# A graph layer and a feed-forward layer on one core: the edges into the first 256 nodes as a dense matrix

## The chip, the core and the metric

The kernel runs on one core of a Trainium2 chip. The metric is the device time of one execution in microseconds (us). The engines are named PE (TensorE), DVE (VectorE), ACT (ScalarE), POOL (GpSimd) and SP (SyncE).

## What is computed

There are 6250 nodes of 256 float32 features and 100,000 weighted edges, sorted by their target node `dst`. The targets are drawn as 6250·u², so they crowd at low node numbers: of the inputs timed here 20,448 edges end in nodes 0 to 255. The sources `src` are spread evenly over all nodes. With `f` the layer-normed rows of `x`:

```python
def _gcn(x, W, b, src, dst, w, n):
    h = x @ W
    return segment_sum(w[:, None] * h[src], dst, n) + b
# graph part, added to x
h  = _gcn(f, W1, b1, src, dst, edge_weight, N)
y  = leaky(concat([h, f[root]], 1))
y  = leaky(_gcn(y, W2, b2, src, dst, edge_weight, N))
x1 = x + leaky(concat([y, h[root]], 1) @ Wl + bl)
# feed-forward part on layernorm(x1): a router picks the best half of the
# nodes; those get gelu(t @ fw1 + fb1) @ fw2 + fb2, times their router weight
```

Since the sum over edges and the product with W can change places, the kernel sums rows first: each of the two graph layers adds up w · row[src] for each target, of `f` in layer 0 and of `y @ W2` in layer 1.

## The kernel before, in words

**Edges as tiles.** The edges are cut into 784 tiles of 128 (`NT`), in the order of `dst`. Four tiles make a group (`TG`), four groups a round (`QG`, `RING` = 16 tiles): 49 rounds (`NIT`) a layer, from the last edges to the first. Nodes are cut into 49 windows of 128 (`NW`). For each tile POOL issues one indirect DMA (L434) that gathers its 128 source rows of 1 KB into the ring in SBUF; DVE makes a selection matrix S of 128×128 (L1153: a column number equals the target within the window, times the edge's weight); PE multiplies S with the rows, four tiles into one PSUM sum (L716, two instruction records a tile); DVE adds the sum to the window's accumulator `acc` (L1161). Where a group's targets reach into the next lower window, it is done again with shifted targets (`S_more`, `dmore`; one extra each time).

**Far tiles.** In every third round one of the 16 tiles is not gathered by POOL. SP fetches its 128 rows with 128 DMAs of one row (L348, in `far_tile`), whose addresses it reads from a table in four loads of 32 registers (L343). PE waits for the tile at its group (`far_ready`, set at L355). There are 16 such tiles a layer and two slots for them.

**Steps.** Once the targets of a window are complete, a step s works on it. In layer 0 a step copies the sum out (ACT, L522), turns it (PE, L789), multiplies it with W1 and W2 (L813, L804) and lets ACT store 128 rows to DRAM (L541); DVE does `z_step0` in the first group of a round and `zero_step0` in the third. In layer 1 a step is the last product, the residual, the layernorm and half of a feed-forward pass over two windows (L854, L865). Steps begin in round `first` (a value computed on the chip, 1 for these inputs), one a round, each engine's pieces tied to the groups of the round (`steps[q]`); those that are left are done behind the rounds.

**Order.** Each engine runs its own stream in order, and semaphores tie them. DVE selects two groups ahead (`select_ahead`), loads a group's window and number of extras from a table into registers (L1180), adds the group before (`add_last`), then frees the ring slot (`group_used`, L1188), for which POOL waits (8 slots of a group, `SLOTS`). PE's sums alternate between two PSUM banks. Between the layers DVE patches the first gathered round with two late windows (L1344), while SP loads `x` again (L331).

Of the kernel before, what the change touches and what calls it, by code (L numbers as in the profile page):

```python
# [17 lines left out]
def gnn_ffn_kernel(nc, x, src, dst, edge_weight, W1, b1, W2, b2, Wl, bl, root_idx,  # L18
# [3 lines left out]
    ds = bass.ds  # L22
# [12 lines left out]
    TG = 4  # L35
    GE = TG * P
    QG = 4
    RING = QG * TG
    SLOTS = 2 * QG
    PADT = RING  # L40
    NIT = -(-E // (RING * P))
    NT = NIT * RING
    NG = NIT * QG
    GR = NG // 2
    CH = 2 * TG
    CR = NT // CH
    SPARE = NT - -(-E // P)
    RAWG = 8
    FAR_EVERY, FAR_Q = 3, 1
    FARS = (NIT - 1) // FAR_EVERY  # L50
    FAR_SLOTS = 2
    FAR_PASS = 32
# [3 lines left out]
    FIRST_EDGE = (NIT - 1) * RING * P  # L56
# [19 lines left out]
    assert NT == CH * CR and NG == 2 * GR and CR == GR <= P and SPARE < TG and 96 < GR and E > 97 * CH * P  # L76
    assert NIT == FARS * FAR_EVERY + 1 and FARS % 2 == 0 and (NW + 1) << CBITS < 1 << SBITS and RAWG < FAR_EVERY * QG
    assert NIT == NW and NACC <= 1 << CBITS

    f_dram = nc.dram_tensor("normed_rows", (NPAD, D), f32).ap()  # L80
# [3 lines left out]
    with ctx:  # L84
# [14 lines left out]
        ring = sb("ring", [P, SLOTS * TG + FAR_SLOTS, D])  # L99
        far = sb("far", [FARS, P], i32)  # L100
        iota = sb("iota", [P, 2 * P], i16)
        idx = sb("idx", [P, NT], i32)
        dstc = sb("dstc", [P, PADT + NT])
        wc = sb("wc", [P, PADT + NT])
        dmore = sb("dmore", [P, TG])
        idx_far = sb("idx_far", [P, FIRST_TILES], i32)
# [41 lines left out]
        wtab = acc[0:1, 1, 0:NG].bitcast(i32)  # L148
        lag = sb("lag", [1, 1], i32)
# [11 lines left out]
        g_lo = stage[:, 0:NG].bitcast(i32)  # L161
        g_hi = rows[:, 0:NG].bitcast(i32)
# [32 lines left out]
        diag = hT[:, :, :].rearrange("p c n -> p (c n)")[:, 0:4 * GR].rearrange("p (a r c) -> p a r c", a=2, c=2)  # L195
# [8 lines left out]
        up_flat = ps_up[:, :, :].rearrange("p c n -> p (c n)")  # L204
        patch_banks = [[up_flat[:, 0:512], up_flat[:, 512:1024]], [ps_h[:, :], ps_o[:, :]]]
# [16 lines left out]
        dve_chain, far_chain = sem("dve_chain"), sem("far_chain")  # L222
# [41 lines left out]
        near_loaded, near_ready, far_listed, zero_stored = sem("near_loaded"), sem("near_ready"), sem("far_listed"), sem("zero_stored")  # L264
        patch_done, patched = sem("patch_done"), [sem(f"patched{q}") for q in range(QG)]
        x_again = sem("x_again")
        raw_stats, raw_second = sem("raw_stats"), sem("raw_second")
# [36 lines left out]
        def _(sp):  # L304
# [24 lines left out]
            def load_x_again():  # L329
# [4 lines left out]
                for r0, r1 in PART:  # L334
                    sp.dma_start(xs[r0:r1, X0 + NW - 1, :], x[(NW - 1) * P + r0:(NW - 1) * P + r1, :]).then_inc(x_again, 16)
# [1166 lines left out]
```

## Time and profile before

| | |
|---|---|
| time of three executions | 2972.7, 2970.2, 2953.6 us, median 2970.2 |
| span of the profiled execution, its own time | 2915.3 us |
| mean granted clock of PE | 0.808 |
| PE / DVE / POOL / ACT busy | 1865.9 / 1169.0 / 1474.9 / 369.1 us |
| records of PE MATMUL / indirect gathers of POOL | 7011 / 1532 |
| bytes moved by DMA | 244.27 MB, mean 84 GB/s |

The span runs from the first to the last instruction; what lies around it in a timed execution is not in the profile. Busy is the union of an engine's instructions; register, branch, semaphore and DMA-issuing instructions are not in it, so an engine can be taken up and not busy. "issue" is time for which the profile shows no wait. A letter q behind an engine means its queue or sequencer.

### The profile page before, as it was taken

How to read it: one execution, taken by the hardware profiler on the slowest of the kernel's cores; microseconds unless marked ns; L12 is line 12 of the kernel's file. 1: busy time of each engine (PE TensorE's matmuls, PEld its weight loads, DVE VectorE, ACT ScalarE, POOL GpSimd, SP SyncE). 2: the span in 40 equal slices, each digit the busy share in tenths (PEclk: the TensorE clock that was granted, in tenths of full speed). 3: DMA queues.
4: the chain of work that ended last, by engine and by line, in shares of the span. 5: the costliest groups of instructions: out<-in, count | busy, mean ns of one | idle time of the engine just before them, and what ended most of it. 6: DMA issues, size and time to landing. Idle time of an engine off the chain costs nothing.

```text
span 2915.3 us, 49425 instructions
## 1 busy us (share of the span) xinstructions
PE 1865.9 (64%) x7011; PEld 1437.8 (49%) x7012; DVE 1169.0 (40%) x4136; ACT 369.1 (13%) x927; POOL 1474.9 (51%) x1571
## 2 busy tenths in 40 slices
PE   0465646655555556354637888886777686757687
PEld 0344535434443444333526666665666465645475
DVE  6543333332332332222324455444544434434356
ACT  4200000000000000000101111111111111111111
POOL 5455555554555554455344555555555554545430
PEclk9788778777776776767878889988988888978797
DMA  6422222222222322222432222222222222222212
GB/s 202 131 83 81 80 80 80 84 78 74 82 81 78 88 79 75 70 79 77 152 98 72 72 72 81 78 79 75 78 81 76 81 71 69 83 62 82 67 50 88
DMA packets 120873, 244.27 MB, mean 84 GB/s; under 512 B 32822, under 2 KB 71046, under 8 KB 120748
## 3 DMA queue, kind: packets, MB, share of 16 engines
q0 software_dynamic: 73664, 200.90, 24.0%
q1 hardware_dynamic: 35612, 32.02, 3.5%
q10 hardware_dynamic: 11472, 10.27, 1.1%
q14 instruction: 117, 0.96, 0.1%
q8 instruction: 8, 0.13, 0.0%
HBM read 223.42 MB, written 19.64 MB: 83 GB/s over the span
## 4 chain that ended last, share of the span: by engine, by line
SPq 53%; issue 35%; PE 5%; DVE 3%; DVEq 1%; another core or an unknown queue 1%; DMA 1%; ACT 1%; ACTq 0%
SPq L348 45%; SPq L343 7%; PE ps_agg L716 2%; PE ps_dn L854 1%; PE ps_up L865 1%; DVE fw2s L1062 1%; DVE S L1153 0%; ACT xs L480 0%; DVE ring L1442 0%; DMA normed_rows<-xs 0%; DVEq L1193 0%; PE ps_o L804 0%; DVE acc L1161 0%; PE ps_dn L852 0%
## 5 line engine op out<-in xcount | busy, mean ns | idle before, releaser
L716 PE MATMUL ps_agg<-ring,S 128*128 x3136 | 912.1, 440 | 677.0 <-SPq L355 320.3
L716 PEld LDWEIGHTS ps_agg<-ring,S 128*128 128x128 f32 x3136 | 669.1, 221 | 860.1 <-issue 757.8
L434 POOL DMA_INDIRECT ring<-conv_rows,idx x752 | 714.5, 950 | 632.4 <-DVEq L1188 424.2
L434 POOL DMA_INDIRECT ring<-normed_rows,idx x736 | 701.1, 953 | 631.7 <-DVEq L1188 426.7
L1153 DVE TENSOR_SCALAR S<-iota,dstc,wc 128x128 f32<-128x128 int16 x1584 | 454.9, 353 | 377.1 <-issue 360.3
L1161 DVE TENSOR_TENSOR acc<-acc,ps_agg x490 | 206.3, 421 | 893.4 <-PE ps_agg L716 478.4
L716 PE MATMUL ps_agg<-ring,S_more 128*128 x768 | 265.7, 506 | 254.6 <-DVE S_more L1153 150.0
L716 PEld LDWEIGHTS ps_agg<-ring,S_more 128*128 128x128 f32 x768 | 187.6, 254 | 321.3 <-issue 287.9
L854 PE MATMUL ps_dn<-fw2s,hT 128*128 128x256 f32 x848 | 232.7, 434 | 0.0
L854 PEld LDWEIGHTS ps_dn<-fw2s,hT 128*128 128x128 f32 x848 | 179.4, 218 | 49.5 <-issue 21.7
L865 PE MATMUL ps_up<-xnT,fw1s 128*128 128x256 f32 x800 | 195.0, 400 | 8.9 <-issue 7.1
L865 PEld LDWEIGHTS ps_up<-xnT,fw1s 128*128 128x128 f32 x800 | 160.7, 204 | 34.5 <-issue 8.1
L1153 DVE TENSOR_SCALAR S_more<-iota,dmore,wc 128x128 f32<-128x128 int16 x384 | 112.7, 365 | 41.2 <-issue 29.2
L522 ACT ACTIVATE stage<-acc 128x256 f32 (+1 forms) x98 | 40.8, 416 | 541.5 <-DVEq L1192 384.0
L532 ACT ACTIVATE xnT<-ps_t 128x256 f32<-128x256 f32 x49 | 18.8, 383 | 611.9 <-PE ps_t L789 480.2
L568 ACT ACTIVATE hT<-ps_up,fb1c 128x256 f32<-128x256 f32 (+1 forms) x212 | 81.9, 472 | 92.2 <-PE ps_up L865 48.6
L548 ACT ACTIVATE yT<-ps_h,b1c 128x128 f32<-128x128 f32 x98 | 30.6, 363 | 326.9 <-remote 245.6
L1143 DVE SCALAR_TENSOR_TENSOR zT<-yT 128x256 f32<-128x256 f32 x99 | 42.1, 425 | 73.9 <-issue 67.9
L789 PE MATMUL ps_t<-ident,stage 128*128 128x128 f32 x196 | 44.9, 317 | 32.4 <-issue 17.2
L804 PE MATMUL ps_o<-W2s,zT 128*128 128x256 f32 x196 | 64.5, 458 | 0.0
L604 ACT ACTIVATE xn<-rows,norm 128x256 f32<-128x256 f32 x48 | 28.8, 600 | 281.7 <-DVE norm L1377 151.0
L813 PEld LDWEIGHTS ps_h<-xnT,W1s 128*128 128x128 f32 x392 | 55.7, 205 | 4.1 <-ACT xnT L532 0.7
(248 smaller groups left out, 1077.2 us busy)
## 6 DMA issues: line engine op xcount, KB each, us to landing
ring<-normed_rows SPq DMA_DIRECT2D x2048, 1.0 KB
ring<-conv_rows SPq DMA_DIRECT2D x2048, 1.0 KB
ring<-conv_rows,idx POOLq DMA_INDIRECT x752
ring<-normed_rows,idx POOLq DMA_INDIRECT x736
conv_rows<-rows ACTq DMA_DIRECT2D x49, 128.0 KB
xs<-in_x SPq DMA_DIRECT2D x6, 640.0 KB
out_rows<-xs SPq DMA_DIRECT2D x3, 1024.0 KB
xs<-in_x SPq DMA_DIRECT2D x2, 1280.0 KB
```

The costliest lines, as they stand in the source:

```text
L343: _, offsets = nc.values_load_multi_w_load_instructions(bass.at_runtime_partition(far[0:1, c * FAR_PASS:(c + 1) * FAR_PASS], k), engines=( ...
L348: sp.dma_start(ring[p:p + 1, SLOTS * TG + b, :].bitcast(i8), rows_of[ds(offsets[i], D * 4)].unsqueeze(0)).then_inc(far_landed[l][b], 16)
L434: pool.indirect_dma_start(out=ring[:, slot * TG + t, :], out_offset=None, in_=rows_of, in_offset=bass.IndirectOffsetOnAxis(ap=at, axis=0)) ...
L568: last = nc.scalar.activation(hT[:, b * HB + c, 0:tokens], ps_up[:, c, 0:tokens], ACT.Gelu_apprx_tanh, bias=fb1c[:, b * HB + c:b * HB + c ...
L716: last = nc.tensor.matmul(to, select[:, t, :], moving, start=(t == 0), stop=(t == TG - 1))
L789: last = nc.tensor.transpose(ps_t[:, k * P:(k + 1) * P], stage[:, k * P:(k + 1) * P], ident[:, :])
L804: last = nc.tensor.matmul(ps_o[:, 0:D], zT[:, k, :], W2s[:, k, :], start=False, stop=(k == KC - 1))
L813: last = nc.tensor.matmul(ps_h[:, c * P:(c + 1) * P], W1s[:, k, c * P:(c + 1) * P], aggT[:, k, :], start=(k == 0), stop=(k == KC - 1))
L854: last = nc.tensor.matmul(ps_dn[:, 0:D], hT[:, c, window * P:(window + 1) * P], fw2s[:, c, :], start=False, stop=(c == HC - 1))
L865: last = nc.tensor.matmul(ps_up[:, c, 0:tokens], fw1s[:, k, (b * HB + c) * P:(b * HB + c + 1) * P], of[:, k, :], start=(k == 0), stop=(k = ...
L1153: last = V.tensor_scalar(to[:, t, :], iota[:, 0:P], at, wc[:, ds(column, 1)], ALU.is_equal, ALU.mult)
L1161: V.tensor_tensor(to, to, flat(ps_agg[:, ds((i + 1) & 1, 1), 0:D]), op=ALU.add).then_inc(acc_step[l], 1)
```

## The change

**Tiles.** The first 160 tiles (`NM`) are taken out of the rounds. Half a tile of padding (`LEAD`) is put ahead of the edges, so that these tiles hold exactly the edges up to node 255. 624 tiles are left: 52 rounds (`NIT`) of three groups (`QG`), with a ring of 6 groups. Far tiles and all of `far_tile` go; POOL gathers all 624 (622 with edges).

**Matrix.** The 160 tiles become a matrix A of 256 targets by all source nodes, held in `xs` (which ACT clears once its rows are stored). In rounds 1 to 40 of layer 0 DVE makes two one-hot matrices for each of four tiles (`hot_tile`: 128×128 of the source within its window, 128×245 of target offset and source window, times the weight), PE multiplies them (`build_tiles`, behind the third group), and a round later DVE adds the 128×245 result to A at a target read from a table (`add_tile`). Rounds 41 to 50 take A and `f` in ten chunks of five windows: SP loads the rows, DVE copies A's chunk (1280 columns a partition), PE makes ten products of 128×128 by 128×256 (`dense_chunk`), and DVE adds them to windows 0 and 1 (`add_chunk`). A is stored to DRAM (6.5 MB in five DMAs of SP). In layer 1 each round begins with one block of A and one window's rows, two DMAs of 128 KB by SP, two products on PE (`dense_block`) and one addition of 512 columns on DVE (`add_block`).

**Rest.** `first` is at least 4 (computed 6 for these inputs, so 46 steps lie in the rounds and two behind them). SP, not ACT, stores a step's rows in layer 0 (`store_rows`). ACT, not SP, loads `x` again, after the patches; DVE waits for it only before the steps. In layer 1 `conv_step1` and `ffn_step_b` share the third group. `select_ahead` comes behind the group's addition, not ahead of it. Should a tile span five targets or more, a general path (`rare_edges`) is taken: 160×49 single products a layer.

```diff
-    QG = 4
+    QG = 3
+    NIT = NW + 3
+    NM = NT - NIT * RING
+    MW = 2
+    SPAN = 5
+    KEYS = SPAN * NW
+    BPER = 4
+    CHUNK = 5
...
 # SP
-            def far_tile(l, rows_of, n, b, before):
-                ...
-                    for i in range(FAR_PASS):
-                        sp.dma_start(ring[p:p + 1, ...], rows_of[ds(offsets[i], D * 4)]...)
+            def store_rows():
+                sp.wait_ge(o_kept[0], s + 2)
+                sp.dma_start(t2_dram[ds(at, P), :], rows[:, :]).then_inc(t2_stored, 16)
+            for i in range(PIECES):
+                sp.dma_start(a_dram[:, w0:w1, :], xs[:, w0:w1, :]).then_inc(matrix_stored, 16)
+            def load_block(i):
+                sp.dma_start(block_a, a_dram[:, a if i < NW else NW, :]).then_inc(block_loaded, 16)
+                sp.wait_ge(t2_stored, 16 * (NW - a + 2))
+                sp.dma_start(block_t, t2_dram[a * P:(a + 1) * P, :]).then_inc(block_loaded, 16)
+            for i in range(1, NIT):
+                sp.wait_ge(block_used, i)
+                load_block(i)
 # ACT
+            act.wait_ge(dense_done, B_IT + CHUNKS)
+            act.wait_ge(matrix_stored, 16 * PIECES)
+            for c, (w0, w1) in enumerate(XCH):
+                act.dma_start(xs[:, X0 + w0:X0 + wf, :], x[w0 * P:wf * P, :]...).then_inc(x_again, 16)
 # PE
+            def build_tiles(it):
+                pe.wait_ge(build_added, it * BPER + (BPER + 1))
+                pe.wait_ge(build_ready, it)
+                for t in range(BPER):
+                    matmul(up_banks[...], src_hot[:, t, :], key_hot[:, t, :])
+            def dense_chunk(it):
+                for m in range(MW):
+                    for k in range(CHUNK):
+                        matmul(to[...], chunk_a[:, k, m * P:(m + 1) * P], blocks[row])
+            def dense_block(it):
+                for m in range(MW):
+                    matmul(to, block_a[:, m * P:(m + 1) * P], block_t)
-            rounds(1, (turn_step1, ffn_step_a, conv_step1, ffn_step_b), ...)
+            rounds(1, ((turn_step1,), (ffn_step_a,), (conv_step1, ffn_step_b)), ...)
 # DVE
+            def hot_tile(it, t):
+                if t == 0:
+                    dve.wait_ge(build_done, it)
+                V.tensor_scalar(src_hot[:, t, :], iota[:, 0:P], src_low[...], None, ALU.is_equal)
+                V.tensor_scalar(key_hot[:, t, :], iota[:, 0:KEYS], keys[...], wc[...], ALU.is_equal, ALU.mult)
+            def add_tile(it, t):
+                base = within(dve.value_load(base_row[0:1, ds(at, 1)]), MSPAN - SPAN)
+                dve.wait_ge(build_done, it)
+                dve.wait_ge(build_added, it * BPER + (t + 1))
+                V.tensor_tensor(to, to, of, op=ALU.add).then_inc(build_added, 1)
             def edge_round(l, it, steps, matrix=None):
                 for q in range(QG):
-                    select_ahead(l, it, q)
                     ... (table load, add_last, group_used)
+                    if matrix == "adds" and q == 0:
+                        with dve.If(it > B_IT):
+                            add_chunk(it, p0 + 2)
                     ... (extras' selections)
+                    select_ahead(l, it, q)
+                    if l == 1 and q == 0:
+                        add_block(p0)
                     ... (window_ready, steps[q])
+                    if matrix and q < 2:
+                        matrix_tiles(it, q, matrix == "adds")
```

## Rows read from the trace of the kernel before

**Rows 1.** The page, part 4: the chain that ended last, by line.

```profile
SPq L348 45%; SPq L343 7%; PE ps_agg L716 2%; PE ps_dn L854 1%; PE ps_up L865 1%; DVE fw2s L1062 1%; DVE S L1153 0%; ACT xs L480 0%; DVE ring L1442 0%; DMA normed_rows<-xs 0%; DVEq L1193 0%; PE ps_o L804 0%; DVE acc L1161 0%; PE ps_dn L852 0%
```

**Rows 2.** The page, part 5: costliest groups, busy, mean, idle before and its releaser.

```profile
L716 PE MATMUL ps_agg<-ring,S 128*128 x3136 | 912.1, 440 | 677.0 <-SPq L355 320.3
...
L434 POOL DMA_INDIRECT ring<-normed_rows,idx x736 | 701.1, 953 | 631.7 <-DVEq L1188 426.7
L1153 DVE TENSOR_SCALAR S<-iota,dstc,wc 128x128 f32<-128x128 int16 x1584 | 454.9, 353 | 377.1 <-issue 360.3
L1161 DVE TENSOR_TENSOR acc<-acc,ps_agg x490 | 206.3, 421 | 893.4 <-PE ps_agg L716 478.4
...
L1153 DVE TENSOR_SCALAR S_more<-iota,dmore,wc 128x128 f32<-128x128 int16 x384 | 112.7, 365 | 41.2 <-issue 29.2
```

**Rows 3.** One line, L348: count, duration ns min/median/max, first and last start.

```profile
L348 SPq DMA_DIRECT2D ring<-normed_rows x2048: 1/225/1390, 88.7 to 1430.6; - x187
...
L348 SPq DMA_DIRECT2D ring<-conv_rows x2048: 2/225/1392, 1459.5 to 2819.3; - x187
```

**Rows 4.** Waits: who waited for whom, us in total, times, longest.

```profile
PE ps_agg L716 <- SPq L355: 320.3, 22, 30.9
```

**Rows 5.** The chain in order of time, 600 to 627 us: start, us, what.

```profile
603.10 2.06 SPq L343
...
607.22 0.22 SPq L348
...
612.96 0.70 SPq L348
```

**Rows 6.** Timeline of POOL, 1108 to 1131: start, us, what, [idle before].

```profile
1114.77 0.94 POOL L434 DMA_INDIRECT ring<-normed_rows,idx  x1 [12.71 <-DVEq L1188]
1116.02 0.94 POOL L434 DMA_INDIRECT ring<-normed_rows,idx  x1 [0.30 <-issue]
```

**Rows 7.** Timeline of DVE, 1406 to 1440 us.

```profile
1408.79 0.42 DVE L1161 TENSOR_TENSOR acc<-acc,ps_agg  x1 [0.38 <-issue]
...
1417.66 0.42 DVE L1161 TENSOR_TENSOR acc<-acc,ps_agg  x1 [3.42 <-issue]
...
1420.15 0.42 DVE L1161 TENSOR_TENSOR acc<-acc,ps_agg  x1 [0.27 <-issue]
...
1425.83 0.42 DVE L1161 TENSOR_TENSOR acc<-acc,ps_agg  x1 [0.39 <-issue]
...
1429.07 0.42 DVE L1161 TENSOR_TENSOR acc<-acc,ps_agg  x1 [0.27 <-issue]
```

**Rows 8.** Stretches: busy us (instructions) of each engine, PEclk, DMA share, GB/s.

```profile
600.00:900.00 300.00, 178.20 (x624) 132.35 (x625) 95.39 (x305) 19.66 (x55) 159.02 (x167) 0.75 0.27 79
...
2811.90:2827.90 16.00, 15.95 (x65) 12.91 (x65) 10.54 (x41) 2.96 (x8) 0.00 (x0) 0.88 0.01 2
2822.40:2838.80 16.40, 16.29 (x78) 13.99 (x77) 10.85 (x41) 4.62 (x12) 0.00 (x0) 1.00 0.00 0
```

**Rows 9.** Timeline of all engines, 608 to 640 us.

```profile
609.16 1.89 PE L716 MATMUL ps_agg<-ring,S 128*128 x8
...
627.09 3.78 PE L716 MATMUL ps_agg<-ring,S 128*128 x8 [1.40 <-DVE acc L1161]
...
629.56 0.29 DVE L1321 COPY acc<-vrow 128x256 f32 x1 [0.36 <-issue]
...
630.36 1.03 POOL L434 DMA_INDIRECT ring<-normed_rows,idx  x1 [0.30 <-issue]
```

**Rows 10.** Timeline of POOL, 1430 to 1500 us.

```profile
1445.30 0.95 POOL L434 DMA_INDIRECT ring<-conv_rows,idx_far  x1 [29.58 <-DMA conv_rows<-rows]
```

**Rows 11.** Timeline of SP, 1440 to 1500 us.

```profile
1459.51 40.46 SPq L348 DMA_DIRECT2D ring<-conv_rows  x47
```

**Rows 12.** Timeline of DVE, 1456 to 1505 us.

```profile
1487.49 0.69 DVE L1344 TENSOR_TENSOR ring<-ring,ps_o 128x512 f32<-128x512 f32 x1 [11.88 <-remote]
```

**Rows 13.** One line, L1180: DVE’s table load at each edge group.

```profile
L1180 DVEq TENSOR_LOAD <-acc x392: 3/305/716, 84.3 to 2836.4; - x196
```

More of the change, by code:

```diff
@@ L513, in rounds @@
                 with act.Fori(0, stop) as s:
-                    for q in range(QG):
-                        steps[q](s)
+                    for piece in steps:
+                        piece(s)
             def stage_sums(l, s):
@@ L748, in rounds @@
+            def rounds(l, steps, stop, ahead_of_steps):
                 pe.reg_mov(extras, 0)
                 pe.reg_mov(step, 0)
-                d = within(pe.snap(first), NIT, 1)
-                with pe.Fori(0, d) as it:
-                    for q in range(QG):
-                        edge_group(l, it, q)
-                if ahead_of_steps is not None:
-                    ahead_of_steps()
+                d = within(pe.snap(first), NIT, NIT - NW + 1)
+                if l == 0:
+                    with pe.Fori(0, 1) as it:
+                        edge_round(l, it, None, None, False)
+                with pe.Fori(1 - l, d) as it:
+                    edge_round(l, it, None)
+                ahead_of_steps()
@@ L765, in rounds @@
                     with pe.Fori(done, stop) as s:
-                        for q in range(QG):
-                            steps[q](s)
-            def no_step(s):
-                pass
+                        for group in steps:
+                            for piece in group:
+                                piece(s)
             def first_root_term():
@@ L781, in _ @@
             pe.sem_inc(raw_second, 1)
[L782 removed]
+            pe.reg_mov(first, pe.value_load(lag[0:1, 0:1], min_val=NIT - NW + 1, max_val=NIT))
             def turn_sums(l, s):
@@ L1242, in rounds @@
                         s = within(dve.snap(step), NIT)
-                        edge_round(l, it, [lambda piece=piece: piece(s) for piece in steps])
+                        edge_round(l, it, [lambda piece=piece: piece(s) for piece in steps], matrix)
                         dve.reg_mov(step, s + 1)
-                end = within(dve.snap(within(dve.snap(extras), NG * NW) + NG), NG * (NW + 1))
+                with dve.Else():
+                    rare_edges(l)
+                end = within(dve.snap(within(dve.snap(extras), NG * NW) + NIT * PER[l]), MOST)
                 done = within(dve.snap(step), NIT - 1)
```

524 lines of the change are left out of this document (340 added, 184 removed).

## The prediction

> **What bounds the kernel now.** I read the chain that ended last first: SP's line L348, the 128 one-row transfers of a far tile, holds 45% of the span, and no compute engine more than a few per cent [rows 1]. The sources of L348 say what to see there: 2048 transfers in each layer, from 88.7 to 1430.6 us and from 1459.5 to 2819.3 us, that is without a break over both layers [rows 3]. 16 tiles in 1342 us are 83.9 us a tile, and a tile comes every third round: 28.0 us a round in layer 0. The groups and waits say who pays: PE stood 320.3 us before L716 for SP's far tile [rows 2, 4], POOL stood 631.7 us in layer 0, mostly for DVE to free a slot, since DVE stood for PE [rows 2].
>
> A far tile should take less. In a quiet stretch one transfer takes 0.22 us (0.32 with its address move and the gaps) and a table load 2.06 [rows 5]: 128 × 0.32 + 4 × 2.1 = 49 us. But beside POOL's packed gathers SP's instructions take 0.70 us each [rows 5]. DVE shows the same: the first group of a round took 3.24 us from addition to addition in a quiet stretch (1425.83 to 1429.07) and 8.87 us in a slow one (1408.79 to 1417.66, with 3.42 us of "issue") [rows 7]. So there are two costs: SP's queue, and a slowing of SP, DVE and PE's sequencer, whose cause I can't read off with certainty.
>
> Below that lie three floors. **POOL:** one gather every 1.25 us when packed [rows 6], so 16 tiles cost 20 us a round. **PE:** four tiles take 1.89 us at full clock and 3.78 at half [rows 9]; the last rounds of layer 1, with neither gathers nor far rows beside them, keep it busy 15.95 of 16.00 and 16.29 of 16.40 us [rows 8]. **DVE:** three quiet groups of layer 0, among them those with the zeroing and with the first step piece, take 8.92 us (1420.15 to 1429.07) [rows 7].
>
> **The change, part by part.** Far tiles: 4096 transfers go, and with them the 28-us pace. SP gets two 128-KB DMAs a round in layer 1 and one in layer 0; a round later they are needed, so I cost them at nothing (cover: a round; without it some 3 us each).
>
> POOL: 1244 gathers in place of 1532, 12 tiles × 1.25 = 15.0 us a round. Over 52 rounds a layer that is 780 us, a floor and not the pace, as follows.
>
> DVE in layer 0, rounds 1 to 40: three groups 8.9 us. Extras: 384 selections are 96 extras, 48 a layer [rows 2]; cut in threes the inputs have 46, 0.9 a round, each four selections (0.28 us each, as L1153's group busy time per instruction), one addition (0.42) and a shift, 1.7 us: 1.5. Matrix: per tile one selection of 128 columns (0.28), one of 245 (no row; between 0.28 and 0.56, I take 0.40, as only the columns grow), one addition of 245 columns from PSUM (0.42 by L1161) with its table load and waits (a quiet plain group of 2.5 us less its selections and addition leaves some 0.9 for all such work; I take 0.5, between 0 and 0.9): 1.6 us, four tiles 6.4, and 0.8 for branches. Sum 17.6 us. DVE also waits at its first `hot_tile` for PE's products, which stand behind PE's step piece of the third group: 0 to 3 us, I take 1.4. With 1 us for what slowing is left: **20 us a round**, above POOL's 15.0 and PE's (three groups 5.7, extras 1.7, build 1.9, step some 3.3 = 12.6 at full clock, 16 at the 0.75 of [rows 8]).
>
> Rounds 41 to 51 of layer 0: DVE's copies and additions are small, but PE has 20 records more (4.7 us), and DVE's `add_chunk` waits for them: 18.5 us, between POOL's 15.0 and 22.
>
> Layer 1, rounds with a step: PE 16.3 [rows 8], less one group 1.9, plus a dense block 0.95, plus extras 1.7 = 17.1 us at full clock. DVE comes to about 16 (16.0 as in [rows 8], less a group 2.5, plus `add_block` 1.4, plus extras 1.5). Two engines this close wait for one another, now that two PE pieces share the third group: I take **20 us**, between 17.1 and 23. Rounds without a step go at POOL's pace, 16 us.
>
> The lag of 6 leaves two steps behind the rounds of each layer; before there were none. No overlap with gathers: some 7 us each in layer 0, 13 in layer 1 (a round of 16 less three quarters of its edge work), 40 us together.
>
> Between the layers: in the old kernel the third group's patch came at 1474.92 and the fourth's at 1487.49 [rows 12], while POOL had begun those gathers at 1445.30 [rows 10] and packed them: 14 × 1.25 us ends at 1463. They landed beside SP's reload of `x`. Now ten tiles land before the reload. From layer 0's last group (some 6 us after SP's last row at 1430.6 [rows 3]) to layer 1's first (some 9 us after the last patch) it was 60 us; I take 10 off. The bounds are 25 off and, if the reload is felt in the rounds, nothing.
>
> SP stores rows where ACT did: one semaphore more in a chain that has a round's time; nothing. Storing A (6.5 MB, five DMAs) and ACT's clearing of `xs` are once each; under 10 us, inside the 18.5 above.
>
> **The sum**, against the profiled execution: layer 0's rounds begin at 84.3 us [rows 13]; first round with set-up 25; 41 × 20 = 820; 10 × 18.5 = 185; two steps 14: 1128. Between the layers 50: 1178. Layer 1: 6 × 16 = 96; 46 × 20 = 920; two steps 26; the tail as before, from the end of the last round (two us behind the last table load at 2836.4 [rows 13]) to 2915.3, 77: 1119. Span 2297 us, against 2915.3. The median of the runs lies 54.9 above the profiled span; kept, that gives **2350 us**, 21% less.
>
> **A rule against the change.** The copy of 256 columns at 629.56 took 0.29 us; the gather that began at 630.36 took 1.03 us, where others take 0.95 [rows 9, 6]. The Trainium skill, "SBUF — State Buffer", section "SBUF: two separate sides", says a float32 copy within SBUF on VectorE locks GpSimd out of writing DMA descriptors; by it the ten `copy_chunk` of 1280 columns, each five times the row's 0.29 us, would stop POOL for up to 15 us in all, and the sum would stay, since POOL has slack there.
>
> **Rivals.**
>
> *The slowing belongs to the gathers, not to SP's rows.* For: it starts and ends with POOL's packed stretches, in the middle of ordinary work of DVE. Against: POOL had been packed from 1445.30 [rows 10] without harm to its neighbours until SP began at 1459.51, and SP then needed 40.46 us for 47 transfers [rows 11], 0.86 each. And POOL will now be paced by fours, with 5 us of gathers in a 6.7-us group. If it stays, I add 3.5 us to each of 51 rounds of layer 0 and 2.5 to each of 46 of layer 1: 179 + 115 = 294, so 2640 us. The Trainium skill, "Perfetto Trace Analysis", section "DMA Instruction — HWDGE (DVE, Sync)", says that these two sequencers share the block that makes descriptors; by that rule DVE's slow stretches would go with SP's transfers, and the time would be that of the forecast. That PE's sequencer is slowed too speaks against its being all.
>
> *The engines overlap better than I allow.* Rounds fall to their bare sums, 17.6 and 17.1: 41 × 2.4 + 10 × 2 + 46 × 2.9 = 252 less, 2100 us. For: PE ran without a gap in the tail [rows 8]. Against: it had no extras there.
>
> *Slower: DVE's matrix work in the slow mode.* Place: DVE's stream in rounds 1 to 40. Price: the slow group is 8.87/3.24 = 2.7 times the quiet one [rows 7]. If POOL, freed of SP's pace, packs its gathers through the whole round, 17.6 us become 48, and layer 0 alone grows by 41 × 28 = 1150 us over the forecast: 3500 us. It decides from 27 us a round in both layers on, that is if more than a third of DVE's work is slow. Against: POOL can't stay packed while it waits for DVE's slots; the two throttle one another.
>
> *The change doesn't do what it says:* the general path is taken. The inputs' last matrix tile spans nodes 251 to 255, inside the five allowed, so it isn't; otherwise many milliseconds.
>
> **How the numbers follow.** Forecast 0.55; slowing stays 0.25; better overlap 0.13; slow matrix work 0.05; general path 0.01; no change within 1% (what a measurement of this kernel can't tell from none) 0.01. The range goes from the better overlap, 2100, to just over the slowing rival, 2660. Faster 0.93, within 1% 0.01, slower 0.06.
>
> **What the changed profile would show.** The chain no longer held by SP but by DVE and PE in turns; L434 with 1244 gathers, no idle time ended by SP; windows of layer 0 with rounds of 20 us, then 18.5, and of layer 1 with 20; PE's granted clock over 0.85 in layer 1; SP's and DVE's 0.70-us instructions gone. Wrong if gathers at 1.25 us fill 95% of a layer (then POOL's floor is the pace), if DVE's "issue" time grows beyond the 377 us of L1153 (the slowing stays), or if DVE waits over 3 us a round at `hot_tile` for `build_tiles`.

## The result

| kernel | median us | lowest to highest | ratio to before, 95% |
|---|---|---|---|
| before | 2971.45 | 2953.6 to 2976.29 | |
| after | 2483.58 | 2475.5 to 2491.61 | 0.838 [0.834, 0.842] |

16% faster. The forecast was 2350 us in a range of 2100 to 2660: right in sign and range, 134 us too low. The profiled execution of the kernel after took 2479.38 us, 1.8 us more than its span.

The page of the kernel after: busy times, the chain by engine, then the groups that answer to [rows 2].

```profile
PE 1820.0 (73%) x7053; PEld 1422.3 (57%) x7054; DVE 1209.6 (49%) x4253; ACT 376.1 (15%) x930; POOL 1205.6 (49%) x1280
...
PE 26%; issue 17%; DVE 14%; DVEq 14%; another core or an unknown queue 4%; POOL 1%; ACT 0%; DMA 0%; ACTq 0%
...
L780 PE MATMUL ps_agg<-ring,S 128*128 (+1 forms) x2496 | 713.4, 437 | 309.8 <-DVE acc L1287 140.5
L484 POOL DMA_INDIRECT ring<-conv_rows,idx x612 | 582.1, 951 | 576.2 <-DVEq L1390 390.4
...
L1287 DVE TENSOR_TENSOR acc<-acc,ps_agg x406 | 170.8, 421 | 604.3 <-issue 268.3
L1279 DVE TENSOR_SCALAR S<-iota,dstc,wc 128x128 f32<-128x128 int16 x1264 | 362.4, 363 | 176.9 <-issue 175.1
```

SP, 52% of the chain by its two lines in [rows 1], has no share left. PE's wait for SP (320.3 us, [rows 4]) is gone, and its idle time before the sums falls from 677 to 310 us. PE and DVE take turns, as forecast, and POOL waits for DVE's slots. But "issue" at DVE's selections is still 175 us (360 before), and 268 at its additions.

Two stretches of 300 us, in the columns of [rows 8]: one of layer 0, one of layer 1.

```profile
600.00:900.00 300.00, 217.04 (x812) 168.03 (x811) 152.41 (x502) 26.95 (x75) 167.74 (x175) 0.80 0.29 82
1300.00:1600.00 300.00, 241.00 (x950) 191.85 (x951) 145.69 (x532) 50.68 (x132) 146.25 (x154) 0.88 0.27 79
```

PE has 217 us of work here where [rows 8] had 178, and POOL is busy 168 of 300 us. No engine is full, so the round is a chain through several.

### The profile page after: what moved, and what is told of

Same layout as the page of the kernel before. It is cut to its first block, busy times and chain, and to the rows that moved or that the text cites. A ratio compares the mean times of both kernels' runs of the same rounds, so it can differ in the third digit from the quotient of the medians.

```text
span 2477.6 us, 40334 instructions
## 1 busy us (share of the span) xinstructions
PE 1820.0 (73%) x7053; PEld 1422.3 (57%) x7054; DVE 1209.6 (49%) x4253; ACT 376.1 (15%) x930; POOL 1205.6 (49%) x1280
## 3 DMA queue, kind: packets, MB, share of 16 engines
q0 software_dynamic: 59808, 163.13, 22.7%
## 4 chain that ended last, share of the span: by engine, by line
PE 26%; issue 17%; DVE 14%; DVEq 14%; another core or an unknown queue 4%; POOL 1%; ACT 0%; DMA 0%; ACTq 0%
PE ps_agg L780 11%; PE ps_dn L979 6%; DVE S L1279 4%; PE ps_up L990 3%; DVEq L1279 2%; DVEq L1377 2%; DVEq L1395 2%; DVE acc L1296 1%; DVEq L1391 1%; DVE S_more L1279 1%; DVEq L1287 1%; PE ps_agg L847 1%; PE ps_dn L977 1%; PE ps_o L1023 1%
## 5 line engine op out<-in xcount | busy, mean ns | idle before, releaser
L780 PE MATMUL ps_agg<-ring,S 128*128 (+1 forms) x2496 | 713.4, 437 | 309.8 <-DVE acc L1287 140.5
L484 POOL DMA_INDIRECT ring<-conv_rows,idx x612 | 582.1, 951 | 576.2 <-DVEq L1390 390.4
L484 POOL DMA_INDIRECT ring<-normed_rows,idx x600 | 576.6, 961 | 489.4 <-DVEq L1390 338.2
L780 PEld LDWEIGHTS ps_agg<-ring,S 128*128 128x128 f32 x2496 | 535.5, 220 | 445.4 <-issue 360.2
L1287 DVE TENSOR_TENSOR acc<-acc,ps_agg x406 | 170.8, 421 | 604.3 <-issue 268.3
L1279 DVE TENSOR_SCALAR S<-iota,dstc,wc 128x128 f32<-128x128 int16 x1264 | 362.4, 363 | 176.9 <-issue 175.1
L780 PE MATMUL ps_agg<-ring,S_more 128*128 (+1 forms) x736 | 264.5, 522 | 215.6 <-DVE S_more L1279 179.6
L780 PEld LDWEIGHTS ps_agg<-ring,S_more 128*128 128x128 f32 x736 | 185.3, 262 | 284.5 <-issue 250.2
L1296 DVE TENSOR_TENSOR acc<-acc,ps_agg 128x512 f32<-128x512 f32 x52 | 35.7, 686 | 157.3 <-PE ps_agg L780 80.5
L813 PE MATMUL ps_up<-hT 128*128 128x245 f32 x320 | 74.4, 375 | 0.0
L1341 DVE TENSOR_TENSOR xs<-xs,ps_up 128x245 f32 x160 | 64.9, 406 | 18.0 <-issue 14.8
```

The lines of the kernel that those rows point to most:

```text
L484: pool.indirect_dma_start(out=ring[:, slot * TG + t, :], out_offset=None, in_=rows_of, in_offset=bass.IndirectOffsetOnAxis(ap=at, axis=0)) ...
L780: last = nc.tensor.matmul(to, select[:, t, :], moving, start=(t == 0), stop=(t == TG - 1))
L813: last = nc.tensor.matmul(up_banks[:, t // 2, t % 2 * KEYS:(t % 2 + 1) * KEYS], src_hot[:, t, :], key_hot[:, t, :], start=True, stop=True)
L1279: last = V.tensor_scalar(to[:, t, :], iota[:, 0:P], at, wc[:, ds(column, 1)], ALU.is_equal, ALU.mult)
L1287: V.tensor_tensor(to, to, flat(ps_agg[:, ds((i + 1) & 1, 1), 0:D]), op=ALU.add).then_inc(acc_step[l], 1)
L1296: V.tensor_tensor(first_acc, first_acc, flat(ps_agg[:, ds((i + 1) & 1, 1), :]), op=ALU.add).then_inc(acc_step[1], 1)
```

## The rounds in every profile

A round here lasts from its first table load on DVE (L1180 in [rows 13], L1377 after) to that of the next; us, means. The last column counts DVE's queue instructions (register, branch, semaphore; no table loads) that took 0.65 to 0.76 us, of some 9,800. Before has 49 rounds of 16 tiles, after 52 of 12; "layer 1" leaves out its first six rounds. The third column is the median of the kernel before in the same comparison.

```
kernel            span    before beside it  layer 0, rounds 6-40  41 on   layer 1   slow on DVE
before            2915.3  (2971)            28.19                 26.60   27.53     577
after             2477.6  2971              20.70                 20.91   22.81     271
b0_before         2976.3  2966              28.76                 27.21   28.36     582
b1_no_far         2647.6  2906              24.70                 23.32   25.38     590
b2_half           2152.9  2906              19.67                 17.77   19.54      92
e2_no_build       2469.5  2966              19.69                 21.41   23.68     281
e7_sp_rows        2489.7  2966              20.68                 20.93   23.07     299
e1_pool_far       2106.3  2071              19.53                 19.90   19.57       0
c1_after          2039.8  2071              15.58                 15.82   20.43       0
e5_half_gathers   2038.0  2071              15.65                 15.19   20.50       0
e8_block_late     1907.1  2071              15.67                 15.06   17.51       0
e9_both_late      1892.3  2071              15.62                 13.89   17.50       0
```

The table holds the chief surprise. The experiments came on five chips, of two kinds: on two the kernel before takes 2906 and 2966 us, on three 2070 to 2071. I call them the slow and the quick kind. Each chip was met in one comparison only, so whether the kind stays with the chip is not shown. The first comparison (2971), and so the result, is of the slow kind. They differ in the last column.

The table also shows how far a column can be trusted. On the quick kind, c1_after and e8_block_late run the same layer 0 and stand at 15.82 and 15.06 in rounds 41 to 50. On the slow kind, after and e2_no_build run the same layer 1 and take 22.81 and 23.68.

## The experiments

### The change on a quick chip

**c1_after** is the kernel after, unchanged.

> The kernel after, unchanged, on the chip of this comparison. Where the kernel before takes about 2071 us, theory (layer 0 is then at GpSimd's 12 x 1.25 = 15 us a round, layer 1 at the 20.3 us of the run with ScalarE's stores, since that run differs from this in layer 0 alone): 2020 to 2045 us, 1 to 3% faster than before. Rival (the stores cost ScalarE's path in layer 0): 1990 to 2015 us. Where the kernel before takes about 2970 us: 2475 to 2495 us.

Measured: 2037.26 us, ratio 0.982 [0.979, 0.986], inside the 2020 to 2045 of its text. So the same change is worth 16% on one kind of chip and 1.8% on the other. One line, L1377, of the first profile and then of this one (count, duration ns min/median/max, first and last start):

```profile
L1377 DVEq FUSED_REGOPS  x204: 4/65/699, 138.8 to 2380.3; - x102
```

```profile
L1377 DVEq FUSED_REGOPS  x204: 57/65/71, 122.3 to 1942.6; - x102
```

The same 204 register instructions have the same median, but on the quick chip none is over 71 ns, and on the slow kind some take 699. Over the program, 271 of 9833 instructions of DVE's queue and 129 of 7335 of PE's are slow in the first, none in the second. DVE's tensor work is nearly equal (1209.6 and 1195.1 us busy). The two executions differ by 438 us of span.

The slow instructions are not the whole of this difference. In rounds 6 to 40 of layer 0, which take 20.70 us and 15.58, DVE's queue instructions take 9.9 us a round and 7.8, PE's 5.7 and 4.9. But PE's products take 14.8 us a round and 12.6, at a granted clock of 0.80 and 0.93. No run takes the clock's part from the rest. Where a price in us a round is put on the slowing below, it is the whole difference between the two chips.

**e4_act_stores** gives the stores back to ACT.

```diff
-                sp.wait_ge(o_kept[0], s + 2)
-                sp.dma_start(t2_dram[ds(at, P), :], rows[:, :]).then_inc(t2_stored, 16)
+                act.wait_ge(o_kept[0], s + 2)
+                act.dma_start(t2_dram[ds(at, P), :], rows[:, :]).then_inc(t2_stored, 16)
```

> The kernel after, with ScalarE waiting for and storing each node tile's rows itself in layer 0, as before the change. My step costed this move at nothing beside the rounds' other work: one transfer and one wait per round on an engine that is busy under 20% of the span. Theory: no difference, 2475 to 2495 us. Rival (ScalarE's next stage stands behind the wait for its own copy, and TensorE behind the stage): 0.3 to 0.8 us in each of 52 rounds, 2500 to 2525 us.

Measured: 2039.39 us, on a quick chip, 2 us from c1_after on another one (before 2070.85 and 2071.05 beside them). Nothing, as costed. Its ratio is 0.987 [0.982, 0.993]; the absolute figures of its text were for the other kind.

### What bounds before and after on a quick chip

**e1_pool_far**: the kernel before, with SP's tiles gathered by POOL.

```diff
-                    by_sp = q == FAR_Q and it > 0 and it % FAR_EVERY == 0
+                    by_sp = False
-                if q == FAR_Q:
-                    pe.wait_ge(far_ready[l], ((it * 171) >> 9) + 1)
 # SP: the far_tile calls go
```

> The kernel before with one thing changed: GpSimd gathers all sixteen tiles of every round, and SyncE fetches no tile row by row. No matrix of far nodes, nothing else of the change. Theory (SyncE's one-row transfers set the rounds before, and the change gains by taking them away): GpSimd now has 16 gathers x 1.25 us = 20.0 us per round as its floor against 15.0 in the kernel after, rounds of 21.5 to 24 us, 104 of them and some 190 us around them: 2430 to 2690 us, most likely 2500, so nearly all of the gain is had without the matrix. Rival (the slowed instructions come with GpSimd's packed queue, not with SyncE's rows): a GpSimd that is the bound is packed all the time, every instruction of VectorE and TensorE's queue goes slow, 2700 to 2950 us.

Measured: 2107.19 us, ratio 1.017 [1.016, 1.019], on a quick chip. The text was written for 2970 us and so can't be judged by its times. But 36.3 us more fits 32 gathers of 1.25 us (40 us), and the rounds stand at 19.5 us. Two lines of it, one per layer:

```profile
L427 POOL DMA_INDIRECT ring<-conv_rows,idx x768 | 738.5, 962 | 235.6 <-issue 229.0 <-DVEq L1179 6.6
L427 POOL DMA_INDIRECT ring<-normed_rows,idx x752 | 717.6, 954 | 248.7 <-issue 219.7 <-DVEq L1179 29.1
```

In layer 0 POOL waits for DVE 29.1 us, where [rows 2] had 426.7, and in layer 1 6.6: it is the bound, always packed, and yet no queue instruction of DVE is slow. Packed gathers alone don't slow the queues. It takes the chip too.

**e5_half_gathers**: the kernel after with half the gathers.

```diff
-                    for t in range(TG):
+                    kept = 2 if it >= 3 else TG
+                    for t in range(kept):
...
-                        pool.indirect_dma_start(...).then_inc(landed[slot // QG][q], 16)
+                        pool.indirect_dma_start(...).then_inc(landed[slot // QG][q], 16 * TG // kept)
```

> The kernel after, with GpSimd issuing two of the four gathers of each group from round 3 of each layer on; what TensorE multiplies for the other two tiles is what the ring held, all else stays. Theory (layer 0's rounds on a quiet chip are GpSimd's 15 us; layer 1's are the chain through the block's product): on a chip where before takes 2071 us, layer 0's rounds fall from 15.7 to 12 to 14.5 us, layer 1's stay within 1 us: 100 to 190 us less than the kernel after. On a chip where before takes 2970 us the packed stretches are half as long, the 0.70-us instructions nearly vanish: 2000 to 2150 us. Rival (VectorE's and TensorE's own work sets the rounds in both layers): less than 50 us gained on the quiet chip.

Measured: 2040.23 us on a quick chip, against 2037.26. My theory fell and its rival stands: layer 0's 15.6 us lie next to POOL's 15.0, but come from DVE and PE. The change had already freed POOL.

### The wait in layer 1

The timeline of the kernel after at a round's start in layer 1, all engines:

```profile
1689.02 3.72 PE L979 MATMUL ps_dn<-fw2s,hT 128*128 128x256 f32 x16
...
1692.58 1.03 PE L847 MATMUL ps_agg<-blocks 128*128 128x256 f32 x4
1695.39 0.69 DVE L1296 TENSOR_TENSOR acc<-acc,ps_agg 128x512 f32<-128x512 f32 x1 [5.72 <-PE ps_agg L780]
...
1696.28 0.42 ACT L582 ACTIVATE stage<-acc 128x256 f32 x1 [6.84 <-DVEq L1408]
...
1696.75 0.44 PE L911 MATMUL ps_t<-ident,stage 128*128 128x128 f32 x2 [1.42 <-ACT stage L582]
```

PE ends the last step piece of the round before (3.72 us), and only then makes the block's product. DVE waits for it with nothing to do ahead of that, idle for 5.72 us. (The row names PE's next group, L780, whose semaphore came 0.30 us behind the block's; the wait in the code is for the block's product, and in c1_after the profile puts all 45 such waits down to L847.) Behind its addition stand `window_ready` and the step piece, for `window_ready` ACT, and for ACT's stage PE. So **e8_block_late** moves the addition down:

```diff
-                    if l == 1 and q == 0:
-                        add_block(p0)
                     if steps and q == 0:
-                        dve.wait_ge(acc_step[l], p0 + 2)
+                        dve.wait_ge(acc_step[l], p0 + 2 - l)
                         dve.sem_inc(window_ready[l], 1)
                     if steps:
                         steps[q]()
+                    if l == 1 and q == 0:
+                        add_block(p0)
```

> The kernel after; in layer 1 alone VectorE opens the window for the node tile's steps and does its step piece ahead of adding the block's product, in place of behind it. Theory (layer 1's rounds of 22.8 us hold a chain of its own: TensorE's last step piece, then the block's product, then VectorE's wait of 5.7 us for it, then ScalarE's stage, then TensorE's turn): the wait leaves the path, rounds of 20 to 21.3 us in 45 rounds, 2375 to 2420 us. Rival (the round is set by the sum of the work and the waits of the twelve gathered tiles, so the wait only moves): 2465 to 2490 us.

Measured: 1915.66 us on a quick chip, 0.927 [0.923, 0.930], 122 us less than c1_after (I had expected 64 to 109 less, for the slow kind), and 124 less than e4_act_stores on the same chip. Layer 1's rounds fall from 20.43 to 17.51 us, layer 0's stay. The addition's idle time in c1_after, then in this run:

```profile
L1296 DVE TENSOR_TENSOR acc<-acc,ps_agg 128x512 f32<-128x512 f32 x52 | 35.7, 686 | 125.5 <-PE ps_agg L847 125.5
```

```profile
L1296 DVE TENSOR_TENSOR acc<-acc,ps_agg 128x512 f32<-128x512 f32 x52 | 35.7, 687 | 47.8 <-PE ps_agg L847 38.4 <-DVE mv L1603 9.4
```

**e9_both_late** moves the dense chunk's addition in layer 0 behind the step piece as well:

```diff
-                    if matrix == "adds" and q == 0:
-                        with dve.If(it > B_IT):
-                            add_chunk(it, p0 + 2)
...
-                        if l == 0:
-                            dve.wait_ge(dense_added, it + 2)
...
                     if l == 1 and q == 0:
                         add_block(p0)
+                    if matrix == "adds" and q == 0:
+                        with dve.If(it > B_IT):
+                            add_chunk(it, p0 + 2)
```

> As the run with the block's addition behind the step piece in layer 1, and in layer 0 also the addition of the dense chunk moved behind the step piece (rounds 41 to 52). Theory: beside the gain of the first, ten rounds of layer 0 lose VectorE's wait of 4.5 us for the dense chunk, 1 to 3 us of each: 10 to 35 us less than that run, 2340 to 2400 us. Rival (layer 0's rounds 41 to 50 are no longer than rounds 6 to 40 for another reason than this wait): no difference from that run within 8 us.

Measured: 1895.97 us, 0.916 [0.914, 0.918], 20 us less than e8_block_late; rounds 41 to 50 fall from 15.1 to 13.9 us, more than the 0.8 us by which two runs of the same code differed there, and to 13.8 in the second run below. That is 12 of the 20 us. This version beats both kernels. In the stretches of layer 1 PE is now nearly full at full clock; one of c1_after, then one of this run:

```profile
1250.00:1550.00 300.00, 258.62 (x1091) 208.11 (x1092) 163.13 (x612) 63.47 (x168) 163.18 (x172) 0.95 0.30 87
```

```profile
1300.00:1600.00 300.00, 288.62 (x1325) 241.17 (x1324) 190.41 (x715) 81.46 (x209) 198.67 (x208) 1.00 0.36 106
```

I ran it once more, as **e9_again**, hoping for a chip of the slow kind:

> The version with both additions moved behind the step piece once more, for a chip on which the kernel before takes about 2900 to 2970 us; on a chip of 2071 us it took 1896. Theory (the 5.7-us wait for the block's product is on the path there too, and queue instructions of 0.70 us come on top as in the kernel after): layer 1's rounds of 22.8 us fall to 20 to 21, layer 0's rounds 41 to 50 from 20.9 to 19.5 or less, 2340 to 2410 us beside 2484, a ratio to before of 0.79 to 0.81. Rival (on such a chip VectorE is the late engine, so that what is taken from its waits is filled with its slowed instructions): 2440 us or more. On a chip where before takes 2071 us: 1890 to 1905 us again.

It came on a quick one: 1903.85 us, 0.920 [0.916, 0.923]. What it brings where before takes 2970 us is not known.

### What the slow kind of chip makes of it

**b0_before**: the kernel before, for its profile.

> The kernel before as it was; only two loads of one number, once per layer, are written with their bounds. It is run for its profile, since the kernel before takes 2071 us on the chips of these experiments and 2970 in the first comparison. Theory (the instructions of 0.70 us of SyncE, VectorE and TensorE's queue belong to the chip, not to the kernel): at about 2071 us there are fewer than 30 of them on SyncE and on VectorE, where the first profile has 665 and 628; a round of 16 tiles lasts GpSimd's gathers, 19 to 19.8 us, where it lasted 28.2; and the run with SyncE's tiles given to GpSimd is longer by just those gathers, 34 x 1.25 = 42 us (36 measured). Rival (the instructions are as slow as before and something else is faster): their counts are above 300 each. At about 2970 us: all is as in the first profile.

It came on a slow chip: one execution, 2978.44 us, rounds as in the first profile, 582 slow instructions on DVE. (The 665 and 628 of its text are those over 0.55 us on SP and DVE, table loads among them; counted as in the table they are 516 and 577.) So there is no profile of before on a quick chip, and that POOL bounds it there rests on e1_pool_far.

**b1_no_far**: no far tiles at all, by anyone.

```diff
 # SP's far_tile calls and PE's wait go, as in e1_pool_far; POOL goes on leaving those tiles out
-                if q == FAR_Q:
-                    pe.wait_ge(far_ready[l], ((it * 171) >> 9) + 1)
```

> The kernel before with SyncE's tiles left out altogether: neither SyncE nor GpSimd fetches the last tile of group 1 in every third round, and TensorE multiplies what its ring slot holds. GpSimd's gathers are as many as before. On a chip where the kernel before takes about 2970 us, theory 1 (the chain of waits runs through SyncE's rows, 320 us of TensorE's wait being for them): 2400 to 2600 us. Theory 2 (the 0.70-us instructions of VectorE and TensorE's queue, which come with GpSimd's packed gathers, are the price, and the rows are only what is late last): 2750 to 2950 us. On a chip where it takes about 2071 us both expect that GpSimd's 16 x 1.25 us a round stay the bound and the rows were free: 2050 to 2080 us; a rival is that the rows cost there too: below 2030 us.

**b2_half**: the rows stay, POOL's gathers are halved.

```diff
-                    for t in range(TG - 1 if by_sp else TG):
+                    kept = 2 if it >= 3 else TG - 1 if by_sp else TG
+                    for t in range(kept):
```

> The kernel before with SyncE's rows as they are, but GpSimd issuing two gathers of each group of four from round 3 of each layer on (TensorE multiplies what the ring holds in place of the others). On a chip where the kernel before takes about 2970 us, theory 2 (packed gathers make SyncE's, VectorE's and TensorE's queue instructions slow, SyncE's rows among them): the counts of 0.70-us instructions fall by half or more, SyncE's tile of rows is no longer late, rounds of 19 to 24 us, 2050 to 2500 us. Theory 1 (SyncE's rows are slow by themselves): SyncE's chain stays, 2750 to 2950 us. On a chip where it takes about 2071 us, theory (GpSimd's gathers set the round of 19.5 us): VectorE's and TensorE's own work shows, 1750 to 1980 us; rival (they set it already, as in the kernel after, where half the gathers gave nothing): 2040 to 2075 us.

Both on one slow chip, before 2905.57 us. Without the rows: 2645.1 us, 0.912 [0.907, 0.917]. With the rows and half the gathers: 2154.49 us, 0.743 [0.738, 0.747]. The first value lies between the two theories, the second is theory 2's, though SP's tile is still late 15 times. One wait of the run without rows; then of the run with half the gathers the chain by line, and one wait:

```profile
DVE S L1144 <- issue: 405.1, 357, 8.6
```

```profile
SPq L348 25%; PE ps_agg L717 10%; SPq L343 6%; PE ps_dn L855 5%; DVE S L1154 3%; PE ps_up L866 3%; DVE acc L1162 1%; DVEq L1154 1%; DVE S_more L1154 1%; PE ps_dn L853 1%; DVEq L1194 1%; PE ps_o L899 1%; DVEq L1162 1%; DVE fw2s L1063 1%
```

```profile
PE ps_agg L717 <- SPq L355: 189.4, 15, 25.1
```

With SP silent, DVE is as slow as ever: 590 slow instructions against 577 and 582, and 405 us of "issue" before its selections (360.3 in [rows 2]). So SP's transfers don't cause the slowing. With half the gathers they fall to 92 on DVE, from 342 to 33 on PE's queue and from 516 to 162 on SP's, with all of SP's rows in place. SP is still 31% of the chain, but 750 us earlier. On such a chip the slowing comes with POOL's gathers. It grows with how deep they are packed. The table gives the share of DVE's queue instructions over 0.55 us (table loads among them), by the place of the gather that ran (begun within 1.3 us) in a row of gathers less than 1.4 us apart, from 100 us on. The last column is of instructions with no gather begun in the 3 us before them, without the one drain at the program's end:

```
place                 1     2     3     4     5     6     7   8 on   (none for 3 us)
before             .016  .028  .045  .114  .321  .551  .517  .640   .000
after              .009  .020  .027  .049  .206  .339  .386  .494   .000
b2_half            .000  .001  .131  .373     (under ten instructions a column)    .000
e1_pool_far, quick .000  .000  .000  .000  .000  .000  .000  .000   .000
```

**e7_sp_rows**: the kernel after, plus SP's rows in layer 1, at addresses fixed when the program is built.

```diff
+                for p in range(42):
+                    sp.dma_start(ring[p:p + 1, SLOTS * TG, :], t2_dram[(p * 131 + i * 17) % N:..., :]).then_inc(rows_in, 16)
```

> The kernel after, with 42 more transfers of one row each by SyncE in every round of layer 1, into a slot of the ring that nothing reads: as many per 12 tiles as the kernel before had for 16. [...] Rival (the rows themselves hinder GpSimd's gathers or VectorE, and so cost time wherever they run): rounds longer by 2 us and more, over 100 us more. On a chip where before takes 2970 us: over 300 us more, with SyncE at 0.3 to 0.9 us a row.

On a slow chip: 2499.79 us, 0.844 [0.840, 0.848], 16 us more than the kernel after; layer 1's rounds 23.07 against 22.81. I had expected over 300 us. SP's queue, 42 rows to a round:

```profile
1516.04 15.31 SPq L421 DMA_DIRECT2D ring<-conv_rows  x42
```

0.36 us a row, where [rows 11] had 0.86; groups of 42 take 12.9 to 18.6 us. From one transfer's start to the next it is 0.36 us in the mean here and 0.64 in the kernel before. The transfer itself did not get cheaper: its instruction takes 0.25 us in the mean and 0.23 before, and 196 of 2142 took over 0.55 us, before 505 of 4096. What a row saves is the second instruction, the address move (518 of 4096 over 0.55 us before), and the table loads. The 0.3 us a round that these rows cost lie within the spread of layer 1 on this kind of chip.

**e2_no_build**: the making of the matrix is left out, its use stays.

```diff
-                V.tensor_scalar(src_hot[:, t, :], ...)
-                last = V.tensor_scalar(key_hot[:, t, :], ...)
+                    dve.sem_inc(build_ready, 1)
-                V.tensor_tensor(to, to, of, op=ALU.add).then_inc(build_added, 1)
+                dve.sem_inc(build_added, 1)
-                    last = nc.tensor.matmul(up_banks[...], src_hot[:, t, :], key_hot[:, t, :], ...)
-                last.then_inc(build_done, 1)
+                pe.sem_inc(build_done, 1)
```

> The kernel after without the making of the matrix in layer 0's first 40 rounds: VectorE's eight hot tiles and four additions per round and TensorE's four products of them are left out, so the matrix stays as it was cleared; its storing, loading and use as dense chunks and blocks stay. My step priced this making at 6.4 us of VectorE per round. Theory (quiet chip: it lies on the path with VectorE's and TensorE's other work, but GpSimd's 12 gathers of 1.25 us stand right behind it): layer 0's rounds go from 15.6 to 15.0 to 15.2 us, 15 to 30 us less than the kernel after. Rival (the making lies in VectorE's idle time and GpSimd is not near): no change within 8 us. Second rival (GpSimd's spacing can close up below 1.25 us): rounds of 12 to 14 us, 60 to 140 us less. On a chip where before takes 2970 us: rounds from 20.7 to 17 or less, over 150 us less.

On a slow chip: 2467.52 us, 0.831 [0.827, 0.834], 16 us less than the kernel after. Layer 0's rounds go from 20.70 to 19.69 us, where I had written 17 or less.

The 16 us hide two larger numbers. Layer 0 is 40 us shorter (1100.8 against 1141.1). Layer 1, which the edit doesn't touch, is 33 us longer (1291.4 against 1258.4), for a reason that no run shows. The pieces left out had taken 4.2 us of DVE a round, so three quarters of what it is spared DVE spends waiting or slowed: its slow instructions in rounds 1 to 40 rise from 126 to 174. On a quick chip this run was not made.

## Why the forecast was right, and where not

**Right: SP's rows leave, and the chain goes to DVE and PE.** b1_no_far prices the rows at 260 us of 2906, beside the 320.3 us that PE waited for them [rows 4]. That is a little over half of the gain (8.8 of 16.2 points). The rest I put down to fewer and less packed gathers; no run shows that at twelve tiles a round. By layers, first load to first load and to the end: 1411.6 to 1141.1 us, and 1419.4 to 1258.4.

**The cause of the slowing was named wrongly.** I priced what is left of it at 1 us a round in layer 0 and at nothing in layer 1, and gave the rival, that it belongs to the gathers, 0.25. Its mechanism holds (b1_no_far, b2_half). By after against c1_after it costs 5.1 us a round in layer 0 and 2.4 in layer 1, near the rival's prices: 3.5 on top of my 1 in layer 0, and 2.5 in layer 1. The lower clock of PE is in these numbers. What spoke against it for me, POOL packed without harm from 1445.30 [rows 10], was between the layers. The part about pacing holds: gathers at the fifth place or deeper fell from 470 to 327, the slow instructions of DVE from 577 to 271.

My signs for it were poor. I wrote that the 0.70-us instructions would be gone; 271 were left on DVE. And I would have seen the slowing stay by an idle time of L1153 beyond 377 us; it stayed while that time fell to 176.9.

The Trainium skill, "Perfetto Trace Analysis", section "DMA Instruction — HWDGE (DVE, Sync)", has the two sequencers share a block that makes descriptors. The rule that I drew from it in the prediction, that DVE's slow stretches go with SP's transfers, is refuted here: DVE's slow instructions stayed with SP silent (590).

**Layer 0: 20 forecast, 20.70 measured, by luck: two errors cancel.** The bare sum was 17.6 us and 1.4 for `hot_tile`'s wait; on the quick chip the round takes 15.6. The matrix's term was the one too large. DVE's pieces for one tile, in layer 0 of e9_both_late, where the matrix is made as in the kernel after:

```profile
512.26 0.28 DVE L1328 TENSOR_SCALAR hT<-iota,routed 128x128 f32<-128x128 int16 x1
...
512.46 0.40 DVE L1329 TENSOR_SCALAR hT<-iota,keys,wc 128x245 f32<-128x245 int16 x1
...
512.81 0.42 DVE L1341 TENSOR_TENSOR xs<-xs,ps_up 128x245 f32 x1
```

The instructions are as long as I took them, but they overlap a little, and the 0.5 us that I gave each tile for its table load and waits is not there: 0.97 us a tile where I had 1.6. In c1_after two tiles take 1.80 us in the mean, so the four take 3.6 us a round (4.2 on the slow kind), not 6.4. The wait at the first `hot_tile`, 1.4 in my sum, is nothing on the quick chip and 0.2 us a round on the slow one. With both set right the sum is 14.8 us, beside 15.6 measured. Against these 4.2 us too many stand the 5.1 us of slowing, where I had 1.

**Rounds 41 to 51: 18.5 forecast, 20.91 measured.** PE's dense chunk and DVE's wait for it were in the sum, but not the step piece and `window_ready` behind that wait. Moving it gives 1.2 us a round on a quick chip. Yet there the rounds take 15.82, less than my 18.5: the miss is the slowing, 5.1 us, for which this sum had no term.

**Layer 1: 20 forecast, 22.81 measured, the largest miss.** It is 126 us over 45 rounds. I had a bare 17.1 us of PE and allowed 2.9 for two engines that wait for one another. On the quick chip the rounds take 20.43, near that 20, and one wait accounts for the allowance: I had named no engine that stands behind `add_block`, and moving it gives 2.9 us (20.43 to 17.51), with 17.5 near my bare 17.1. So the term that failed is the slowing, at nothing in this sum: 22.81 against 20.43, 2.4 of the 2.8 us missed. What the wait costs on the slow kind no run shows. The rounds without a step took 20.0 us, not POOL's 16, 24 us more; on the quick chip they take 12.6, so that miss too is of the slow kind.

**The frame.** The first round took 36.1 us, not 25; layer 0 began at 78.1, not 84.3. The span came to 2477.6, 181 above my sum: 41 by layer 1's start, 139 in layer 1. The 54.9 us that I kept between span and median hid part of that and were a misreading: a timed execution is about 2 us longer than its own span. The profiled one of before, 2915.3 us, was shorter than all seven timed ones of the 2966 chip and all four beside the result, and lies in the range of the 2906 chip (2884.71 to 2926.51); on which chip it ran isn't recorded. One detail of the change: the 160 tiles hold 160 × 128 − 64 = 20,416 edges, so the last 32 edges into node 255 are still gathered.

**The slower rival** didn't come about: the round stayed at 20.7, under its 27. POOL's waits for DVE (390 us in layer 1, 338 in layer 0) show the throttling that I had put against it.

**The copy's rule.** The timeline of the kernel after, at one of the ten copies:

```profile
1019.91 1.16 POOL L484 DMA_INDIRECT ring<-normed_rows,idx  x1 [0.30 <-issue]
1020.14 0.81 DVE L1347 COPY hT<-xs 128x1280 f32 x1
```

The gather took 1.16 us, where its neighbours take 0.94 and 0.95, and this is one of the mildest cases. Nine of the ten copies met a gather, and these nine took 1.15 to 1.43 us, each ending 0.12 us after its copy. The copy took 0.81 us, not five times 0.29. Together they cost POOL 2.8 us, where the rule's reading in the prediction had up to 15, and nothing in the sum. By the Trainium skill's "SBUF: two separate sides" (page "SBUF — State Buffer") such a copy locks GpSimd out of writing descriptors; gathers that end only behind the copy agree with it.

## What to carry to other kernels

When a change adds a wait to an in-order engine, write down what stands behind it in that queue, and who waits for that: an addition that nobody needed at once held ACT's and PE's next step, and moving it three lines down gave 6% on a quick chip, more than the whole change had given there. If a profile has register instructions at ten times their median, ask what the time would be without them before costing anything by slowed rows: a sum can come out right with two wrong terms. And a gain that comes from escaping such a slowing holds for the chip it was measured on; measure it on a second one.

## What was not expected of the hardware

- Chips differ by 900 us on one program: 2906 to 2971 us on some and 2071 on others, at 577 and more against 0 slow queue instructions (for the quick chips by the kernels run there). The same change gives 16% on one and 1.8% on the other.
- On the slow kind, some queue instructions of SP, DVE and PE take 0.70 us in place of 0.04 to 0.07 while POOL's indirect gathers run deep (DVE: 0.02 of them at the first gather of a row, 0.64 at the eighth and later); ACT's never (0 of 1325 and 1227). DMA packets are no slower: POOL's queue has 22.7% of 2477.6 us and 27.8% of 2039.8 us, 562 and 567 us.
- One-row DMAs with fixed addresses go at 0.36 us each on such a chip; 42 of them in a round lengthened it by 0.3 us, no more than two runs of the same code differ.
- Nine gathers that ran when a 0.8-us float32 copy began on DVE each ended 0.12 us after it.

Open: what makes a chip one kind or the other, and whether it stays so; how much of the difference is PE's lower clock; by what path gathers slow the other queues; what the rows cost before on a quick chip; and the best version's time on the slow kind.
